# Queries kept once and unscaled, and scaled per head on GpSimd beside the attention

## The chip, the cores and the metric

The kernel runs on one core of a Trainium2 chip. The metric is device time in microseconds (us) of one execution. The core has five engines that run side by side: TensorE (matrix products), VectorE and ScalarE (elementwise work), GpSimd (general), and SyncE, whose queue issues nearly all transfers (DMAs) here.

## The reference

Input x is (8, 1024, 256). The first part is an attention without a softmax: each of 16 heads of 16 dimensions sums five sines of the scaled product of query and key, and a sigmoid makes the weight.

```python
q = (x @ Wq.T + bq).reshape(B, L, H, hd).transpose(0, 2, 1, 3)   # k, v alike
sim = jnp.einsum('bhid,bhjd->bhij', q, k) / jnp.sqrt(hd)
sim = sim / (jnp.abs(temperature)[0] + 0.1)
scores = 0
for fi, freq in enumerate([31.0, 37.0, 41.0, 43.0, 47.0]):
    scores = scores + alpha[:, fi] * jnp.sin(TWO_PI * sim / freq + phi[:, fi])
w = jax.nn.sigmoid(scores)
w = w / (jnp.sum(w, axis=-1, keepdims=True) + 1e-10)
out = layernorm(einsum('bhij,bhjd->bhid', w, v) @ Wo.T + bo) * gamma + beta
x = layernorm(x + out)
```

A second part picks 127 of 1024 rows of each batch entry with a router, runs a transformer block on them, puts them back, and ends with another layer normalization. The change doesn't touch it.

## The kernel before

The program has three blocks, one after the other, which hand data on through HBM: `project_qkv`, `oscillatory_attention`, `routed_block`. Between engines there are semaphores only, each engine's instructions run in the order in which they are written.

**Projections.** A loop over 8 batch entries. TensorE turns x (L200), ScalarE draws it from PSUM (L346), TensorE makes queries and keys (L211) and values (L219). VectorE draws the queries, scaled by temperature (L306), sums x (L310), adds the bias to the values (L318) and splits the keys in a rounded part, the rest and both negated (L326 to L331). The query also has to be divided by each of the five periods and split in a rounded part and a rest, so that products in TensorE's reduced fp32 format (fp32r) stay exact: `split_q` does it on VectorE for five frequencies, with ten operations for each half of the 256 dimensions (L296, L300) and ten writes of 1 MB in all to `q_d`, which has the shape [B, 2, D, NF, L]. SyncE's `keep` issues these writes (L141); each of five buffers is taken again once its write has landed (`q_kept`). A table `tab_d` holds for each head the amplitudes, the reciprocal periods and the phases in two parts.

**Attention.** 128 heads (8 batch entries by 16), one after the other, with two sets of buffers. For a head, `q_r` holds for each frequency and half of the queries 51 rows: 16 dimensions of the rounded part, these again, 16 of the rest, two phase rows and a row of ones. SyncE's `load` brings these rows from `q_d` and from `ph_d`, an array of phase rows made by VectorE at the start, and the keys' rows from `k_d`. `k_r` holds the keys for it, `rounder` the constants by which the sum is brought to a whole number of turns and taken away again. The keys are taken in 8 units of 128. For each unit and frequency TensorE makes one group of eight matmuls into one of three PSUM slots (`fill`, L527; two halves of the array side by side), ScalarE takes the sine (L593), and for each pair of units VectorE sums the five sines, weighted, in four operations (L609). ScalarE turns the sum into a weight with a Tanh (L587), TensorE multiplies by the values (L547), VectorE draws the result (L618). GpSimd only copies a head's five amplitudes (L506).

What orders the work: ScalarE may be at most a pair ahead of VectorE (`summed`: two buffers of sines, and the Tanh of one pair stands before the last sine of the next). TensorE is at most three sines ahead of ScalarE. The loads of a head's keys and queries wait until the fills of the head before last, which used the same buffers, are done (`filled`).

Elsewhere, in the routed block, GpSimd also does a 128x2048 `tensor_tensor` for each batch entry (L800), at times beside VectorE's work (L1087, L1088). These lines serve as a measure below.

Of the kernel before, what the change touches and what calls it, by code (L numbers as in the profile page):

```python
# [15 lines left out]
F32R = mybir.dt.float32r  # L16
# [60 lines left out]
def project_qkv(nc, x, wq, bq, wk, bk, wv, bv, temperature, alpha, phi, q_d, k_d, v_d, vs_d, tab_d):  # L77

    with ExitStack() as ctx:
# [10 lines left out]
        rate = sb("p_rate", [P, KC, NF])  # L90
# [6 lines left out]
        q_hl = sb("p_q_hl", [P, NF, 2, L])  # L97
# [10 lines left out]
        q_kept = [sem(f"q_kept{f}") for f in range(NF)]  # L108
        k_kept, v_kept = sem("k_kept"), sem("v_kept")
        q_step, q_split, k_step, k_split = sem("q_step"), sem("q_split"), sem("k_step"), sem("k_split")  # L110
        tab_in, tab_step, tab_done, tab_kept, rate_in = sem("tab_in"), sem("tab_step"), sem("tab_done"), sem("tab_kept"), sem("rate_in")
        totals, tot_ready, tot_kept = sem("totals"), sem("tot_ready"), sem("tot_kept")

        with nc.Block() as block:

            @block.sync
            def _(sp):
# [9 lines left out]
                for f in range(NF):  # L127
                    sp.sem_inc(q_kept[f], 16)
# [6 lines left out]
                def keep(b):  # L135
                    sp.wait_ge(v_ready, b + 2)
                    sp.dma_start(v_d[b, :, :, :], v_sb[:]).then_inc(v_kept, 16)
                    for m in range(KC):
                        for f in range(NF):
                            sp.wait_ge(q_split, NF * (KC * b + m) + f + 1)  # L140
                            sp.dma_start(q_d[b, :, m * P:(m + 1) * P, f, :].rearrange("i p l -> p i l"),  # L141
                                         q_hl[:, f, :, :]).then_inc(q_kept[f], 16)
# [9 lines left out]
                for m in range(KC):  # L152
                    sp.dma_start(rate[:, m, :], tab_d[8 * m:8 * m + 8, 1, :].unsqueeze(1).broadcast_to([8, HD, NF])).then_inc(rate_in, 16)
# [10 lines left out]
                for f in range(NF):  # L164
                    sp.wait_ge(q_kept[f], 16 * (KC * B + 1))
# [66 lines left out]
            def _(dve):  # L232
# [58 lines left out]
                def split_q(b, m):  # L291

                    whole = qk_sb[:, 0, m, :]
                    for f in range(NF):
# [3 lines left out]
                    for f in range(NF):  # L298
                        dve.wait_ge(q_step, NF * (KC * b + m) + f + 1)
                        nc.vector.scalar_tensor_tensor(q_hl[:, f, 1, :].bitcast(F32R), whole, rate[:, m, f:f + 1],  # L300
                                                       q_hl[:, f, 0, :], ALU.mult, ALU.subtract).then_inc(q_split, 1)

                with dve.Fori(0, B, 1) as b:
                    dve.wait_ge(q_summed, b + 1)
                    for m in range(KC):
# [6 lines left out]
                    dve.wait_ge(q_ready, b + 1)  # L312
                    dve.wait_ge(rate_in, 32)
                    split_q(b, 0)
# [7 lines left out]
                    split_q(b, 1)  # L322
# [35 lines left out]
def oscillatory_attention(nc, tab_d, q_d, k_d, v_d, ph_d, o_d):  # L358
# [3 lines left out]
    HF = H * NF  # L362
    with ExitStack() as ctx:
# [4 lines left out]
        phase = sb("a_phase", [HF, 2])  # L368
        phase_rows = sb("a_phase_rows", [HF, 2, L])
        fixed = sb("a_fixed", [2, 2, L])  # L370
        fixed_m = sb("a_fixed_m", [1, 3, HALF])
# [12 lines left out]
        table_in, phase_step, phase_kept = sem("table_in"), sem("phase_step"), sem("phase_kept")  # L384
        setup, cleared, fixed_in = sem("a_setup"), sem("a_cleared"), sem("a_fixed_in")
        qk_loaded = [sem("qk_loaded0"), sem("qk_loaded1")]
# [27 lines left out]
        LOADS = 16 * 14  # L414
# [11 lines left out]
        with nc.Block() as block:  # L426

            @block.sync
            def _(sp):
                sp.dma_start(table[:],  # L430
                             tab_d[:, 0, :].partition_broadcast(P)).then_inc(table_in, 16)
                for i in range(2):
                    sp.dma_start(phase[:, i:i + 1], tab_d[:, 2 + i, :].rearrange("h (f o) -> h f o", o=1),
                                 allow_slow_non_contiguous=True).then_inc(table_in, 16)
                sp.wait_ge(cleared, 9)
                for j in range(2):
                    at = 64 * j + ONE_ROW
                    for i in range(2):
                        sp.dma_start(rounder[at:at + 1, i, :], fixed_m[:, i, 0:P]).then_inc(fixed_in, 16)
                    for k in range(2):  # L440
                        for i in range(2):
                            sp.dma_start(k_r[64 * j + 48:64 * j + 50, k, i, :], fixed[:, i, :]).then_inc(fixed_in, 16)
                        sp.dma_start(q_r[at:at + 1, k, :, :], fixed_m[:, 2:3, :].broadcast_to([1, NF, HALF])).then_inc(fixed_in, 16)
                sp.wait_ge(phase_step, 2)
                sp.dma_start(ph_d.rearrange("i h f l -> (h f) i l"), phase_rows[:]).then_inc(phase_kept, 16)
                sp.wait_ge(phase_kept, 16)

                def load(g, k):

                    wait_pos(sp, filled, NF * U * (g - 1))  # L450
                    b, h = g // H, g % H
                    to_q = lambda row, count, src: sp.dma_start(q_r[row:row + count, k, :, :], src).then_inc(qk_loaded[k], 16)
# [31 lines left out]
            def _(pool):  # L484
# [7 lines left out]
                for i, value in enumerate((ROUND, -ROUND, 1.0)):  # L492
                    last = nc.gpsimd.memset(fixed_m[:, i, :], value)
# [789 lines left out]
```

## Time and profile before

| | |
|---|---|
| runs shown | 7113.47, 7120.93, 7120.65 us, median 7120.65 |
| profiled execution | 7119.98 us, its span (first to last instruction) 7118.2 us |
| TensorE, matmul | 6113.5 us busy, 86% |
| ScalarE | 5853.0 us, 82% |
| VectorE | 5773.2 us, 81% |
| GpSimd | 205.8 us, 3% |
| moved by DMA | 446.10 MB |

The busy shares are averages over three blocks with different limits; each is to be read by itself. PE is TensorE, DVE VectorE, ACT ScalarE, POOL GpSimd, SP SyncE.

### The profile page before, as it was taken

How to read it: one execution, taken by the hardware profiler on the slowest of the kernel's cores; microseconds unless marked ns; L12 is line 12 of the kernel's file. 1: busy time of each engine (PE TensorE's matmuls, PEld its weight loads, DVE VectorE, ACT ScalarE, POOL GpSimd, SP SyncE). 2: the span in 40 equal slices, each digit the busy share in tenths (PEclk: the TensorE clock that was granted, in tenths of full speed). 3: DMA queues.
4: the chain of work that ended last, by engine and by line, in shares of the span. 5: the costliest groups of instructions: out<-in, count | busy, mean ns of one | idle time of the engine just before them, and what ended most of it. 6: DMA issues, size and time to landing. Idle time of an engine off the chain costs nothing. (4 is left out here: it accounts for less than half of the span.)

```text
span 7118.2 us, 130314 instructions
## 1 busy us (share of the span) xinstructions
PE 6113.5 (86%) x48057; PEld 4363.9 (61%) x48057; DVE 5773.2 (81%) x4353; ACT 5853.0 (82%) x5874; POOL 205.8 (3%) x217
## 2 busy tenths in 40 slices
PE   6539999999999999999999999999999999826555
PEld 3326666666666666666666666666666666625444
DVE  6648888888888888888888888888888888857775
ACT  1139999999999999999999999999999999901111
POOL 0000000000000000000000000000000000010000
PEclk8769999999999999999999999999999999966666
DMA  7931111111111111111111111111111111131220
GB/s 291 358 143 47 47 47 46 46 47 46 45 47 45 45 47 47 47 46 47 46 47 46 47 47 46 47 45 46 47 45 46 47 45 47 30 81 46 50 52 20
DMA packets 322961, 446.10 MB, mean 63 GB/s; under 512 B 158980, under 2 KB 189604, under 8 KB 321384
## 3 DMA queue, kind: packets, MB, share of 16 engines
q1 hardware_dynamic: 317032, 432.81, 19.4%
q8 instruction: 422, 6.91, 0.4%
q0 software_dynamic: 5376, 5.30, 0.3%
q14 instruction: 131, 1.07, 0.0%
HBM read 284.11 MB, written 153.75 MB: 62 GB/s over the span
## 5 line engine op out<-in xcount | busy, mean ns | idle before, releaser
L593 ACT ACTIVATE a_wave<-a_ps_turn 128x1024 f32<-128x1024 f32 x5120 | 4915.0, 1365 | 132.2 <-PE a_ps_turn L527 131.9
L527 PE MATMUL a_ps_turn<-a_q_r,a_k_r 64*128 64x512 f32 x20480 | 3392.0, 399 | 399.8 <-ACT a_wave L593 249.3
L609 DVE SCALAR_TENSOR_TENSOR a_weight<-a_wave,a_head_c,a_weight 128x2048 f32<-128x2048 f32 x1536 | 3612.6, 2352 | 59.5
L527 PE MATMUL a_ps_turn<-a_q_r,a_rounder 64*128 64x512 f32 x20480 | 3241.4, 392 | 4.6 <-issue 4.6
L527 PEld LDWEIGHTS a_ps_turn<-a_q_r,a_k_r 64*128 64x128 f32 x20480 | 1951.8, 185 | 1574.9 <-ACT a_wave L593 804.5
L527 PEld LDWEIGHTS a_ps_turn<-a_q_r,a_rounder 64*128 64x128 f32 x20480 | 1976.6, 186 | 244.6 <-issue 9.4
L609 DVE SCALAR_TENSOR_TENSOR a_weight<-a_wave,a_head_c 128x2048 f32<-128x2048 f32 x512 | 1203.9, 2351 | 844.4 <-ACT a_wave L593 844.4
L587 ACT ACTIVATE a_weight<-a_weight,a_head_c 128x2048 f32<-128x2048 f32 x512 | 1186.0, 2316 | 5.2 <-DVE a_weight L609 5.2
L547 PE MATMUL a_ps_out<-a_weight,a_v_r 128*32 128x512 f32 x4096 | 547.2, 606 | 7.6 <-ACT a_weight L587 5.4
L506 POOL COPY a_head_c<-a_table 128x5 f32 (+1 forms) x128 | 114.3, 893 | 5596.2 <-ACT a_weight L587 5596.1
L547 PEld LDWEIGHTS a_ps_out<-a_weight,a_v_r 128*32 128x32 f32 x4096 | 80.8, 108 | 194.7 <-issue 184.0
L352 ACT ACTIVATE p_qk_sb<-p_lo,p_bias 128x1024 f32<-128x1024 f32 x16 | 16.9, 1110 | 220.1 <-DVE p_k_hl L331 203.8
L219 PE MATMUL p_hi<-p_w_t,p_x_t 128*128 128x256 f32 x256 | 71.0, 446 | 108.0 <-DVE p_qk_sb L306 108.0
L296 DVE TENSOR_SCALAR p_q_hl<-p_qk_sb,p_rate 128x1024 fp32r<-128x1024 f32 x80 | 57.3, 749 | 112.4 <-DMA q_d<-p_q_hl 112.4
L219 PEld LDWEIGHTS p_hi<-p_w_t,p_x_t 128*128 128x128 f32 x256 | 58.0, 230 | 124.2 <-DVE p_qk_sb L306 113.8
L917 PE MATMUL Bk<-ident,logits 128*127 128x128 f32 x128 | 30.3, 431 | 117.9 <-ACT logits L965 117.9
L965 ACT ACTIVATE spread<-spread 128x8 f32<-128x8 f32 x24 | 5.0, 209 | 137.0 <-DVE spread L1052 136.9
L917 PEld LDWEIGHTS Bk<-ident,logits 128*127 128x127 f32 x128 | 27.9, 334 | 120.1 <-ACT logits L965 120.1
L211 PE MATMUL p_hi<-p_x_t,p_w_t 128*128 128x512 f32 x128 | 73.4, 738 | 27.7 <-ACT p_x_t L346 16.9
L300 DVE SCALAR_TENSOR_TENSOR p_q_hl<-p_qk_sb,p_rate,p_q_hl 128x1024 fp32r<-128x1024 f32 x80 | 97.0, 1277 | 0.0
L858 PE MATMUL A<-woa_t,o_t 128*128 128x256 f32 x256 | 69.7, 433 | 27.8 <-DVE o_t L1081 27.8
L618 DVE COPY a_out<-a_ps_out 128x512 f32<-128x512 f32 x128 | 87.4, 683 | 4.1 <-PE a_ps_out L547 4.1
(231 smaller groups left out, 1919.3 us busy)
## 6 DMA issues: line engine op xcount, KB each, us to landing
q_d<-p_q_hl SPq DMA_DIRECT2D x80, 1024.0 KB, 8.3
a_q_r<-q_d SPq DMA_DIRECT2D x256, 320.0 KB
a_k_r<-k_d SPq DMA_DIRECT2D x512, 128.0 KB
a_q_r<-q_d SPq DMA_DIRECT2D x256, 160.0 KB
k_d<-p_k_hl SPq DMA_DIRECT2D x8, 4096.0 KB, 15.2
a_k_r<-k_d SPq DMA_DIRECT2D x512, 64.0 KB
o_d<-a_out SPq DMA_DIRECT2D x512, 34.0 KB
num<-o_d SPq DMA_DIRECT2D x32, 512.0 KB
```

The costliest lines, as they stand in the source:

```text
L211: last = nc.tensor.matmul(out[:, 2 * m + half, :], w_t[:, n, c, m * P:(m + 1) * P], x_t[:, c, half * HALF:(half + 1) * HALF], start=(c == ...
L219: last = nc.tensor.matmul(hi[:, t // 2, (t % 2) * D:(t % 2 + 1) * D], x_t[:, c, t * P:(t + 1) * P], w_t[:, 2, c, :], start=(c == 0), stop= ...
L300: nc.vector.scalar_tensor_tensor(q_hl[:, f, 1, :].bitcast(F32R), whole, rate[:, m, f:f + 1], q_hl[:, f, 0, :], ALU.mult, ALU.subtract).the ...
L506: nc.gpsimd.tensor_copy(head_c[:, k, :], table[:, bass.ds(g % H, 1), :].rearrange("p h f -> p (h f)")).then_inc(const_ready, 1)
L527: last = nc.tensor.matmul(ps_turn[slot_of(r, s, f)][:, half, :], exact(w(rows[half])), exact(q_r[rows[half], k, f, :]), start=(i == 0), st ...
L547: last = nc.tensor.matmul(ps_out[VP * c:VP * (c + 1), :], v_r[:, k, t + c // 2, :], weight[:, t // 2, c // 2, halved(c % 2)], start=(t == ...
L587: nc.scalar.activation(tile, tile, ACT.Tanh, scale=head_c[:, k if s > 1 else 1 - k, 0:1]).then_inc(squashed, 1)
L593: nc.scalar.activation(wave[:, s // 2 % 2, f, s % 2, :], ps_turn[slot_of(r, s, f)][:].rearrange("p a b -> p (a b)"), ACT.Sin, scale=TURN_I ...
L609: return v.scalar_tensor_tensor(both(weight[:, i, :, :]), both(wave[:, i % 2, f, :, :]), head_c[:, k, f:f + 1], to, ALU.mult, ALU.add)
L618: v.tensor_copy(out[:, 1 - k, :], ps_out[:]).then_inc(out_ready, 1)
L858: ins = mm(A[:, 2 + t // 2, (t % 2) * D:(t % 2 + 1) * D], o_t[:, c, half * HALF + t * P:half * HALF + (t + 1) * P], woa_t[:, c, :], start= ...
L917: ins = tr(Bk[0:KSEL, n // 4, (n % 4) * P:(n % 4 + 1) * P], logits[:, n, 0:KSEL], ident[:])
```

## The change

The queries are written once, unscaled: `q_d` becomes [B, D, L], one write of 1 MB for each batch entry, and `split_q` goes from the projections, with its buffers and the `rate` table. In attention a head's 16 rows of queries are loaded three times over into a small tile `q_in`, [P, 2, HALF]; its rows 48 to 50 (and 112 to 114) are ones. A tile `factor` holds for each row and head the five factors by which its row of `q_in` is to be multiplied: the reciprocal periods, the two parts of the phase, and a one. A new `split_q` on GpSimd makes a head's whole `q_r` a head ahead. The phase rows in HBM, VectorE's work for them and their loads go. TensorE waits for `q_ready` beside the keys' loads.

```diff
-                def split_q(b, m):
-
-                    whole = qk_sb[:, 0, m, :]
-                    for f in range(NF):
-                        dve.wait_ge(q_kept[f], 16 * (KC * b + m + 1))
-                        nc.vector.tensor_scalar(q_hl[:, f, 0, :].bitcast(F32R), whole, rate[:, m, f:f + 1], None,
-                                                ALU.mult).then_inc(q_step, 1)
-                    for f in range(NF):
-                        dve.wait_ge(q_step, NF * (KC * b + m) + f + 1)
-                        nc.vector.scalar_tensor_tensor(q_hl[:, f, 1, :].bitcast(F32R), whole, rate[:, m, f:f + 1],
-                                                       q_hl[:, f, 0, :], ALU.mult, ALU.subtract).then_inc(q_split, 1)
...
+                    for k in range(2):
...
+                        sp.dma_start(q_in[64 * j + 48:64 * j + ONE_ROW + 1, k, :], fixed[0:1, 0:1, 0:HALF].broadcast_to([1, 3, HALF])).then_inc(fixed_in, 16)
+                    sp.dma_start(factor[64 * j:64 * j + 48, :, :], tab_d[:, 1, :].partition_broadcast(48)).then_inc(table_in, 16)
+                    for i in range(2):
+                        sp.dma_start(factor[64 * j + 48 + i:64 * j + 49 + i, :, :], tab_d[:, 2 + i, :].partition_broadcast(1)).then_inc(table_in, 16)
+                    sp.dma_start(factor[at:at + 1, :, :].rearrange("p h f -> p (h f)"), fixed[0:1, 0, 0:H * NF]).then_inc(table_in, 16)
...
                 def load(g, k):
+                    wait_pos(sp, q_taken, g - 1)
+                    for j in range(2):
+                        sp.dma_start(q_in[64 * j:64 * j + 48, k, :],
+                                     q_d[b, dims, halved(j)].unsqueeze(0).broadcast_to([3, HD, HALF])).then_inc(q_loaded[k], 16)
                     wait_pos(sp, filled, NF * U * (g - 1))
...
-                        to_q(64 * j, 2 * HD, q_d[b, 0:1, dims, :, halved(j)].broadcast_to([2, HD, NF, HALF]))
-                        to_q(64 * j + 2 * HD, HD, q_d[b, 1, dims, :, halved(j)])
-                        to_q(64 * j + 3 * HD, 2, ph_d[:, head, :, halved(j)].rearrange("i o f l -> i (o f) l"))
...
+                def split_q(g, k):
+
+                    nc.gpsimd.tensor_copy(rate[:, k, :], factor[:, bass.ds(g % H, 1), :].rearrange("p h f -> p (h f)")).then_inc(rate_ready, 1)
+                    pool.wait_ge(rate_ready, g + 1)
+                    pool.wait_ge(q_loaded[k], q_loads(g, k))
+                    whole = q_in[:, k, :].unsqueeze(1).broadcast_to([P, NF, HALF])
+                    scale = rate[:, k, :].unsqueeze(2).broadcast_to([P, NF, HALF])
+                    nc.gpsimd.tensor_tensor(q_all[:], whole, scale, ALU.mult).then_inc(q_step, 1)
+                    wait_pos(pool, filled, NF * U * (g - 1))
+                    nc.gpsimd.tensor_tensor(q_r[:, k, :, :].bitcast(F32R), whole, scale, ALU.mult).then_inc(q_taken, 1)
+                    pool.wait_ge(q_step, g + 1)
+                    pool.wait_ge(q_taken, g + 1)
+                    for j in range(2):
+                        low = slice(64 * j + 32, 64 * j + 48)
+                        last = nc.gpsimd.tensor_tensor(q_r[low, k, :, :].bitcast(F32R), q_all[low, :, :], q_r[low, k, :, :], ALU.subtract)
+                    last.then_inc(q_ready, 1)
+                    pool.wait_ge(q_ready, g + 1)
...
                 def body(g, k):
                     if not isinstance(g, int) or g + 1 < HEADS:
+                        split_q(g + 1, 1 - k)
                         constants(g + 1, 1 - k)
...
-                dve.wait_ge(table_in, 48)
-                for i in range(2):
-                    v.tensor_copy(phase_rows[:, i, :].bitcast(F32R), phase[:, i:i + 1].broadcast_to([HF, L])).then_inc(phase_step, 1)
```

## Rows read from the trace of the kernel before

**Rows 1.** The page: busy tenths of each engine in 40 equal slices.

```profile
PE   6539999999999999999999999999999999826555
DVE  6648888888888888888888888888888888857775
ACT  1139999999999999999999999999999999901111
```

**Rows 2.** Windows: one head, attention, its cold start, projections (batch 0, later), attention's preparation.

```profile
core 0: us, PE busy (x) PEld busy (x) DVE busy (x) ACT busy (x) POOL busy (x), PEclk, DMA share, GB/s
1015.77:1059.95 44.18, 42.22 (x356) 29.73 (x352) 38.24 (x18) 44.18 (x45) 0.91 (x2) 1.00 0.16 47
...
473.20:479.00 5.80, 5.80 (x28) 4.94 (x30) 0.00 (x0) 2.32 (x3) 0.00 (x0) 0.50 0.24 71
20.52:48.78 28.26, 24.88 (x81) 14.73 (x81) 16.47 (x17) 5.28 (x4) 0.00 (x0) 1.00 0.11 41
240.00:285.00 45.00, 26.59 (x80) 15.90 (x79) 31.74 (x30) 5.28 (x4) 0.00 (x0) 0.77 0.94 364
412.40:473.20 60.80, 0.00 (x0) 0.03 (x1) 2.45 (x2) 1.49 (x2) 13.35 (x14) 0.50 0.18 46
473.20:6220.60 5747.40, 5438.35 (x45052) 3836.26 (x45056) 4892.58 (x2175) 5660.49 (x5632) 113.95 (x126) 0.99 0.16 46
```

**Rows 3.** Timeline of one pair: start us, us, engine, line, operation [idle before].

```profile
1011.90 2.35 DVE L609 SCALAR_TENSOR_TENSOR a_weight<-a_wave,a_head_c 128x2048 f32<-128x2048 f32 x1 [1.52 <-ACT a_wave L593]
...
1014.29 7.12 DVE L609 SCALAR_TENSOR_TENSOR a_weight<-a_wave,a_head_c,a_weight 128x2048 f32<-128x2048 f32 x3
...
1015.77 0.91 POOL L506 COPY a_head_c<-a_table 128x5 f32 x1 [43.25 <-ACT a_weight L587]
```

**Rows 4.** The page, projections: groups (busy us, mean ns | idle), and DMA issues.

```profile
L296 DVE TENSOR_SCALAR p_q_hl<-p_qk_sb,p_rate 128x1024 fp32r<-128x1024 f32 x80 | 57.3, 749 | 112.4 <-DMA q_d<-p_q_hl 112.4
...
L300 DVE SCALAR_TENSOR_TENSOR p_q_hl<-p_qk_sb,p_rate,p_q_hl 128x1024 fp32r<-128x1024 f32 x80 | 97.0, 1277 | 0.0
...
q_d<-p_q_hl SPq DMA_DIRECT2D x80, 1024.0 KB, 8.3
...
k_d<-p_k_hl SPq DMA_DIRECT2D x8, 4096.0 KB, 15.2
```

**Rows 5.** Timeline of the first batch's projections, TensorE.

```profile
20.52 9.36 PE L211 MATMUL p_hi<-p_x_t,p_w_t 128*128 128x512 f32 x16 [3.39 <-ACT p_x_t L346]
...
43.49 1.91 PE L200 MATMUL p_lo<-p_ident,p_x_in 128*128 128x128 f32 x16
48.78 8.83 PE L211 MATMUL p_hi<-p_x_t,p_w_t 128*128 128x512 f32 x16 [3.38 <-ACT p_x_t L346]
```

**Rows 6.** Timeline, one small issue on SyncE's queue before attention.

```profile
430.52 0.73 SPq L443 DMA_DIRECT2D a_q_r<-a_fixed_m  x1
```

**Rows 7.** Timeline in the routed block, GpSimd beside VectorE.

```profile
6349.89 1.37 POOL L819 DMA_INDIRECT m_row<-in_L_ffn_attention_mask,mask_row  x1 [0.17 <-issue]
...
6350.51 5.45 DVE L1087 TENSOR_TENSOR den<-den 128x128 f32<-128x128 f32 x1
6351.30 4.51 POOL L800 TENSOR_TENSOR x_in<-x_in,rows 128x2048 f32<-128x2048 f32 x1
```

**Rows 8.** Groups of GpSimd's instructions: busy us, mean ns | idle before.

```profile
L783 POOL TENSOR_SCALAR_AFFINE_SELECT spot<-spot 128x1024 f32<-128x1024 f32 x2 | 3.0, 1518 | 0.0
```

**Rows 9.** Tile a_head_c: duration ns min/median/max, first and last start.

```profile
L609 DVE SCALAR_TENSOR_TENSOR a_weight<-a_wave,a_head_c,a_weight x1536: 2350/2352/2355, 486.2 to 6216.0; 128x2048 f32<-128x2048 f32 x192
...
L506 POOL COPY a_head_c<-a_table x128: 178/903/1222, 425.9 to 6135.1; 128x5 f32 x122, 128x5 f32<-128x5 f32 x6
```

**Rows 10.** Lines L1087 and L1088: duration ns min/median/max.

```profile
L1087 DVE TENSOR_TENSOR den<-den x8: 291/292/5449, 6272.1 to 6946.4; 128x128 f32<-128x128 f32 x8
...
L1088 DVE TENSOR_SCALAR den<-den x8: 226/226/4401, 6272.4 to 6946.7; 128x128 f32<-128x128 f32 x8
```

**Rows 11.** Timeline of attention's first sines on ScalarE.

```profile
477.02 1.02 ACT L593 ACTIVATE a_wave<-a_ps_turn 128x1024 f32<-128x1024 f32 x1 [0.68 <-PE a_ps_turn L527]
```

More of the change, by code:

```diff
@@ L107, in project_qkv @@
         q_ready, k_ready, v_ready = sem("q_ready"), sem("k_ready"), sem("v_ready")
[L108 to L111, printed above, removed]
+        q_kept, k_kept, v_kept = sem("q_kept"), sem("k_kept"), sem("v_kept")
+        k_step, k_split = sem("k_step"), sem("k_split")
+        tab_in, tab_step, tab_done, tab_kept = sem("tab_in"), sem("tab_step"), sem("tab_done"), sem("tab_kept")
         totals, tot_ready, tot_kept = sem("totals"), sem("tot_ready"), sem("tot_kept")
@@ L135, in keep @@
                 def keep(b):
+                    sp.wait_ge(q_ready, b + 1)
+                    sp.dma_start(q_d[b, :, :].rearrange("(m p) l -> p m l", p=P), qk_sb[:, 0, :, :]).then_inc(q_kept, 16)
                     sp.wait_ge(v_ready, b + 2)
                     sp.dma_start(v_d[b, :, :, :], v_sb[:]).then_inc(v_kept, 16)
-                    for m in range(KC):
-                        for f in range(NF):
-                            sp.wait_ge(q_split, NF * (KC * b + m) + f + 1)
-                            sp.dma_start(q_d[b, :, m * P:(m + 1) * P, f, :].rearrange("i p l -> p i l"),
-                                         q_hl[:, f, :, :]).then_inc(q_kept[f], 16)
                     sp.wait_ge(k_split, b + 2)
@@ L163, in _ @@
                 sp.dma_start(vs_d[:, :, :], v_tot[:]).then_inc(tot_kept, 16)
-                for f in range(NF):
-                    sp.wait_ge(q_kept[f], 16 * (KC * B + 1))
+                sp.wait_ge(q_kept, 16 * (B + 1))
                 sp.wait_ge(k_kept, 16 * (B + 1))
@@ L289, in _ @@
                 flat = lambda ap: ap.rearrange("p m l -> p (m l)")
[L291 to L301 removed]
                 with dve.Fori(0, B, 1) as b:
                     dve.wait_ge(q_summed, b + 1)
+                    dve.wait_ge(q_kept, 16 * (b + 1))
                     for m in range(KC):
@@ L367, in oscillatory_attention @@
         table = sb("a_table", [P, H, NF])
-        phase = sb("a_phase", [HF, 2])
-        phase_rows = sb("a_phase_rows", [HF, 2, L])
+        factor = sb("a_factor", [P, H, NF])
+        rate = sb("a_rate", [P, 2, NF])
+        q_in = sb("a_q_in", [P, 2, HALF])
+        q_all = sb("a_q_all", [P, NF, HALF])
         fixed = sb("a_fixed", [2, 2, L])
-        fixed_m = sb("a_fixed_m", [1, 3, HALF])
+        fixed_m = sb("a_fixed_m", [1, 2, P])
         rounder = sb("a_rounder", [P, 2, P])
@@ L491, in _ @@
                 pool.wait_ge(setup, 1)
-                for i, value in enumerate((ROUND, -ROUND, 1.0)):
+                for i, value in enumerate((ROUND, -ROUND)):
                     last = nc.gpsimd.memset(fixed_m[:, i, :], value)
```

55 lines of the change are left out of this document (23 added, 32 removed).

## The prediction

> **What bounds the kernel now.** I read the page by slices first [rows 1]. Three stages show: slices 1 to 3 (projections), slices 4 to 35 (attention) and the last five (routed block). In the middle stage ScalarE and TensorE are at 9 tenths and VectorE at 8, so three engines lie close together. The windows [rows 2] put numbers on it: in one head of 44.18 us ScalarE is busy for all of it, TensorE for 42.2 and VectorE for 38.2; the whole attention stage takes 5747.4 us, 44.9 us for each of 128 heads. ScalarE sets the pace and VectorE has 6 us of slack. The reader should see how thin that is: anything that takes more than some 6 us from VectorE in a head makes VectorE the bound.
>
> The timeline of one pair of key blocks [rows 3] shows how. VectorE does four scalar_tensor_tensor of 128x2048 (one of 2.35 us, then three in 7.12), then waits 1.5 us for a sine. With the hand-overs a pair is 9.55 us of VectorE against 11.04 of ScalarE (a quarter of a head). A head is 38.2 us busy [rows 2] plus 16 gaps of 0.035, so 38.8 us of VectorE.
>
> In the projections the windows show 45 us for a batch, DMA at 0.94 and 364 GB/s, TensorE at 27 us and VectorE at 32 [rows 2]. VectorE's scaled queries wait 112 us for the writes of the scaled queries, 80 of 1 MB each [rows 4]. DMA bounds this stage.
>
> **What is removed.** In a batch, ten scalings and ten subtractions, (57.3 + 97.0) / 8 = 19.3 us of VectorE [rows 4], and nine of ten MB written, 9.4 MB. Of 364 GB/s x 45 us = 16.4 MB that leaves 7.0 MB, 19 us. VectorE keeps 31.7 - 19.3 = 12.4 us. What is late next is TensorE's chain with ScalarE's draw of the turned input: batch 0, where no write had yet filled the queue, ran from 20.52 to the next batch's first matmul at 48.78, 28.26 us, TensorE 24.9 busy at full clock [rows 2, 5]. Eight such batches from 20.5, less the last batch's turning and draw (1.9 + 3.4 [rows 5]), end at 241.3. Some two thirds of VectorE's 12.4 us (adding to values, splitting keys) follow, 8.3, and the last keys' write, 15.2 to landing [rows 4]: 264.8. The stage ended at 412.4 before, so **-147.6 us**. Bounds: at DMA's 19 us for a batch it would be another -74; if TensorE stays at the later window's clock of 0.77 [rows 2], its 24.9 us become 32.3 and the gain falls to -88.
>
> The 256 loads of scaled queries of 320 and 256 of 160 KB and the phase loads go too, three SyncE issues of each half for one small one. DMA in a head is at 0.16 [rows 2] and no head waits for it: 0 us, hidden behind 44 us of ScalarE.
>
> **The start of attention** took 60.8 us before the first matmul [rows 2]. Clearing falls from 13.4 to about 8.8 us on GpSimd (5120 columns become 1104). SyncE then issues 24 small DMAs for 16, at about 0.68 (one shown is 0.73 [rows 6]): 16.3. The phase rows' way through HBM is gone. New on the path are the first query load (1.4 to issue, about 4 to land) and GpSimd's split of head 0, 16.8 as below. Sum 47.3, so **-13.5 us** (-8 with the long subtraction).
>
> **What is added.** For each head GpSimd does one 5-column copy, two products 128x2560 and two subtractions of 16 partitions by 2560. A two-input tensor_tensor on GpSimd took 4.51 us at 2048 columns [rows 7]: 2.2 ns a column, 5.6 us at 2560. GpSimd's own time, 17 to 22 us in a head of 44, has room, and the queries are ready a head ahead of TensorE. If that were all, it would cost 0.
>
> It is not all. The trace of before shows the two engines stopping each other. GpSimd's 5-column copy is 178 ns at the least and 903 in the median [rows 9]: the one at 1015.77 started within a VectorE operation begun at 1014.29, and ended at 1016.68, within 0.04 us of that operation's end at 1016.64 [rows 3]. In the other direction, VectorE's 128x128 tensor_tensor, 292 ns in the median, took 5449 ns once [rows 10]: begun at 6350.51, it ended at 6355.96, just behind GpSimd's two-input product (6351.30 + 4.51 = 6355.81) [rows 7]. A one-input operation beside another such product was stretched from 226 to 4401 ns [rows 10]. So a GpSimd product holds VectorE for its whole length, and attention's 16 operations have the same form, two inputs in SBUF.
>
> The page "SBUF — State Buffer" of the Trainium skill, section Who interferes with whom, says the same against this change: a VectorE instruction with two SBUF inputs and a GpSimd instruction that reads SBUF exclude each other for their full length. By that rule, the trace agrees, with 5449 ns for 292.
>
> The holds per head are two products, 11.2 us, and the subtractions. These touch partitions 32 to 47 and 96 to 111, with no wait between them. No row shows two such operations. Bounds: 5.6 (side by side) and 11.2 (in turn). The nearest is the same stretch [rows 7]: VectorE's short operation was held from 6350.51, though the product is shown only from 6351.30, behind an indirect DMA; something of the product may already have run. That speaks weakly for GpSimd work overlapping, and I take 5.6: holds of 16.8 us.
>
> The page "GPSIMD Engine Reference" of the skill, section Instruction dispatch, says that each of eight cores serves 16 partitions and starts the next instruction when its own share is done; by it the holds would be 16.8 too. No row here can show it.
>
> Now VectorE is the bound: 38.8 + 16.8 = 55.6 us. On top comes what it still waits for ScalarE: in the pairs without a hold it works at 11.04 instead of 9.55, 1.5 us each. Two such pairs would give 3.0, against 0 if the holds leave ScalarE far enough ahead. I take 2.4: **58.0 us per head**. 128 x 58.0, less the 16.8 the last head has no use for, is 7407 us, against 5747: **+1660 us**. The odd 0.7 us between 44.18 and 44.9 lies within ScalarE's new idle time.
>
> Sum: 7118.2 - 147.6 - 13.5 + 1660 = 8617.1, and with the 1.8 us that lie around the span 8619. The profiled execution, 7119.98, is 0.7 below the median of the runs, 7120.65. So +21%. About 0.2% is what a measurement of this kernel can tell from no change.
>
> **Rivals.**
> (a) The subtractions run in turn: 5.6 us more in each of 128 splits, +717: 9336 us. For it: all other GpSimd operations in the trace follow one another. Against: the held operation above.
> (b) The products are cheaper, because an operand that repeats isn't fetched for each column. A one-input selection of 1024 columns took 1.5 us [rows 8], 3.75 at 2560. Holds 7.5 + 5.6 = 13.1, head 54.3: 8149 us.
> (c) The other side: VectorE isn't held. GpSimd takes the port only in VectorE's gaps, or attention's operation goes through while a product waits. Then both savings stand alone: 7118.2 - 161.1 + 1.8 = 6959 us. It decides as soon as holds are under 6.1 us of slack plus 161 / 128 = 1.3, so 7.4 us in a head. For it: in 126 heads GpSimd's copy waited and VectorE's 2352 ns never moved (2350 to 2355) [rows 9]; but that copy is too short to hold anything. Against: the held operations [rows 7, 10].
> (d) TensorE's clock. It was granted 0.50 of full speed, 1.2 GHz, when it began after 61 us of idleness [rows 2], and a group of eight matmuls then took 1.70 us [rows 11] where ScalarE asks for one each 0.96. A head at this level would be 40 x 1.70 + 4 x 2.1 = 76 us, above 58: about 10,900 us. It decides if the mean granted clock falls under 42.2 / 58 = 0.73. Against: TensorE stays busy over 70% and ScalarE stops only for some 8 us at a time. A short dip at half clock, for which ScalarE has spare time, costs nothing in my sum.
> (e) No difference. The change does what it says, but gain and loss cancel: that takes the 7.4 us of holds named in (c), which no row gives.
>
> **How the numbers follow.** Forecast 0.50, (a) 0.23, (b) 0.13, (c) 0.08, (d) 0.04, (e) within 0.2% 0.02. The forecast's own range is 8310 (no wait for ScalarE) to 8750. The range reaches to (b) at 8140 and to (a) with 0.8 us more of waits, 9440; it leaves out (c), (d), (e) and some. Faster 0.08, same 0.02, slower 0.90.
>
> **What would show it.** In the profile after: VectorE's scalar_tensor_tensor with a median near 2352 but a mean well above (16.8 us over 16: about 3.4 us), maxima near 8; GpSimd's products near 5.6 plus up to 2.35 of waiting; ScalarE's busy share in attention down to 0.76, VectorE's nearly 1; period of a head 58. The two subtractions starting within 0.2 us of each other speak for 16.8, one 5.6 behind the other for (a). Attention's first matmul near 312, not 473. TensorE's clock in the windows of attention near 0.9 or above; below 0.73 it is (d). The prediction is wrong if VectorE's operations keep 2352 as their mean.

## The result, and the profile of the changed kernel

The changed kernel takes 9022.88 us (median of four runs, 9016.48 to 9023.65) against 7117.99 in runs beside them: a ratio of 1.2675, interval [1.2653, 1.2697]. The forecast was 8619 us, 8140 to 9440. Direction and range hold, and the point is 4.5% low. The range holds only because it reaches to rival (a): the forecast's own part of it, 8310 to 8750, doesn't contain the result. The profiled execution (9016.48, span 9014.7) is used below.

From the page, busy time of each engine, then tenths of it in 40 slices, as in [rows 1]:

```profile
PE 6392.0 (71%) x48057; PEld 4661.3 (52%) x48057; DVE 7894.1 (88%) x4191; ACT 5916.5 (66%) x5874; POOL 3696.2 (41%) x857
...
PE   8577777777777777777777777777777777764555
...
DVE  4599999999999999999999999999999999976776
ACT  1477777777777777777777777777777777771111
POOL 0444544444444454444445445444444544520000
```

ScalarE and TensorE fall from 9 tenths to 7 and VectorE rises to 9: in attention VectorE is now the bound. The windows (columns as in [rows 2]) of projections, the start of attention, attention, one head, and three stretches of that head:

```profile
20.00:256.00 236.00, 194.51 (x632) 115.55 (x632) 104.20 (x82) 39.31 (x31) 0.00 (x0) 0.90 0.62 237
256.70:308.00 51.30, 0.00 (x0) 0.02 (x1) 0.00 (x0) 1.49 (x2) 27.80 (x18) 0.50 0.19 42
308.00:8086.00 7778.00, 5736.27 (x45056) 4146.21 (x45056) 7149.61 (x2175) 5723.95 (x5632) 3589.75 (x763) 0.87 0.07 20
3038.00:3099.30 61.30, 45.00 (x354) 32.00 (x353) 56.06 (x17) 44.68 (x45) 28.17 (x7) 0.86 0.07 20
3048.00:3064.00 16.00, 5.47 (x48) 3.47 (x44) 15.93 (x3) 3.13 (x4) 15.38 (x3) 0.81 0.05 18
3064.00:3076.00 12.00, 7.28 (x38) 5.74 (x40) 11.04 (x5) 8.25 (x8) 2.24 (x2) 0.55 0.00 0
3076.00:3087.00 11.00, 10.85 (x94) 7.77 (x93) 9.35 (x5) 11.00 (x12) 0.00 (x0) 1.00 0.07 7
```

Attention takes 7778 us, 60.8 a head (this head 61.3), where it was 5747 [rows 2]. The first matmul comes at 308.0 instead of 473.2. VectorE does the same 2175 operations as before and is busy for 7149.6 us instead of 4892.6. The page's groups show on which, with what GpSimd now does:

```profile
L608 DVE SCALAR_TENSOR_TENSOR a_weight<-a_wave,a_head_c,a_weight 128x2048 f32<-128x2048 f32 x1536 | 5453.0, 3550 | 59.9 <-DVE a_weight L608 0.5
...
L608 DVE SCALAR_TENSOR_TENSOR a_weight<-a_wave,a_head_c 128x2048 f32<-128x2048 f32 x512 | 1630.1, 3184 | 627.4 <-ACT a_wave L596 627.4
L491 POOL TENSOR_TENSOR a_q_all<-a_q_in,a_rate 128x2560 f32<-128x2560 f32 x128 | 572.9, 4476 | 3489.2 <-DMA a_q_in<-q_d 3489.1
L498 POOL TENSOR_TENSOR a_q_r<-a_q_all,a_q_r 16x2560 fp32r<-16x2560 f32 x256 | 1919.0, 7496 | 25.8
L493 POOL TENSOR_TENSOR a_q_r<-a_q_in,a_rate 128x2560 fp32r<-128x2560 f32 x128 | 827.6, 6466 | 26.4 <-PE a_ps_turn L528 26.4
```

VectorE's sums (L608) take (5453.0 + 1630.1) / 128 = 55.3 us a head instead of 16 x 2.35 = 37.6. That is 17.7 us of holds. GpSimd's means hold its own waiting too. The timeline just before the first matmul, with VectorE idle, shows its operations alone (start, length):

```profile
287.67 4.46 POOL L491 TENSOR_TENSOR a_q_all<-a_q_in,a_rate 128x2560 f32<-128x2560 f32 x1 [4.02 <-DMA a_q_in<-q_d]
292.08 4.45 POOL L493 TENSOR_TENSOR a_q_r<-a_q_in,a_rate 128x2560 fp32r<-128x2560 f32 x1
296.68 11.19 POOL L498 TENSOR_TENSOR a_q_r<-a_q_all,a_q_r 16x2560 fp32r<-16x2560 f32 x2
```

A product takes 4.45 us, not 5.6. The two subtractions take 11.19 us together: in turn, 5.6 each. The same in the head of the window, GpSimd and VectorE:

```profile
3037.43 4.46 POOL L491 TENSOR_TENSOR a_q_all<-a_q_in,a_rate 128x2560 f32<-128x2560 f32 x1 [28.30 <-DMA a_q_in<-q_d]
3041.84 6.51 POOL L493 TENSOR_TENSOR a_q_r<-a_q_in,a_rate 128x2560 fp32r<-128x2560 f32 x1
3048.50 15.08 POOL L498 TENSOR_TENSOR a_q_r<-a_q_all,a_q_r 16x2560 fp32r<-16x2560 f32 x2
```

```profile
3038.29 5.75 DVE L608 SCALAR_TENSOR_TENSOR a_weight<-a_wave,a_head_c 128x2048 f32<-128x2048 f32 x1 [1.53 <-ACT a_wave L596]
3044.07 21.65 DVE L608 SCALAR_TENSOR_TENSOR a_weight<-a_wave,a_head_c,a_weight 128x2048 f32<-128x2048 f32 x3
3065.65 2.34 DVE L608 SCALAR_TENSOR_TENSOR a_weight<-a_wave,a_head_c 128x2048 f32<-128x2048 f32 x1
...
3077.55 2.35 DVE L608 SCALAR_TENSOR_TENSOR a_weight<-a_wave,a_head_c 128x2048 f32<-128x2048 f32 x1 [2.40 <-ACT a_wave L596]
```

The engines alternate. VectorE's first operation waits for L491's end (2.35 becomes 5.75), the next three take 21.65 us instead of 7.13, and each of GpSimd's later operations waits up to 2.1 us for the VectorE operation in progress (6.51 - 4.45; 15.08 - 11.19 for two). ScalarE's timeline shows what that does further on:

```profile
3041.66 9.47 ACT L596 ACTIVATE a_wave<-a_ps_turn 128x1024 f32<-128x1024 f32 x10
3065.76 2.00 ACT L590 ACTIVATE a_weight<-a_weight,a_head_c 128x2048 f32<-128x2048 f32 x1 [14.63 <-DVE a_weight L608]
3067.67 2.83 ACT L596 ACTIVATE a_wave<-a_ps_turn 128x1024 f32<-128x1024 f32 x3
3070.84 1.02 ACT L596 ACTIVATE a_wave<-a_ps_turn 128x1024 f32<-128x1024 f32 x1 [0.34 <-PE a_ps_turn L528]
3072.55 1.02 ACT L596 ACTIVATE a_wave<-a_ps_turn 128x1024 f32<-128x1024 f32 x1 [0.68 <-PE a_ps_turn L528]
3074.26 1.02 ACT L596 ACTIVATE a_wave<-a_ps_turn 128x1024 f32<-128x1024 f32 x1 [0.68 <-PE a_ps_turn L528]
3075.56 3.79 ACT L596 ACTIVATE a_wave<-a_ps_turn 128x1024 f32<-128x1024 f32 x4 [0.28 <-PE a_ps_turn L528]
```

ScalarE fills its buffers and stands for 14.6 us, TensorE with it (5.5 us busy in 16). For the 12 us behind it TensorE's granted clock is 0.55, close to the lower level of 1.2 GHz, and for a while sines come 1.71 us apart. The ten sines from 3067.67 on take 11.7 us; the ten of the next pair, at full clock, take 9.25. VectorE, just released, then waits for a sine, 2.40 us here. So a head is 38.8 us of VectorE's own + 17.7 of holds + 4.4 of waiting ((627.4 less one wait of 72.4 before the first head) / 127) = 60.9.

### The profile page after: what moved, and what is told of

It reads as the page before. It is cut to its first block and busy times, and to the rows that moved or that the text cites. A ratio compares the mean times of both kernels' runs of the same rounds, so it can differ in the third digit from the quotient of the medians.

```text
span 9014.7 us, 129841 instructions
## 1 busy us (share of the span) xinstructions
PE 6392.0 (71%) x48057; PEld 4661.3 (52%) x48057; DVE 7894.1 (88%) x4191; ACT 5916.5 (66%) x5874; POOL 3696.2 (41%) x857
## 5 line engine op out<-in xcount | busy, mean ns | idle before, releaser
L608 DVE SCALAR_TENSOR_TENSOR a_weight<-a_wave,a_head_c,a_weight 128x2048 f32<-128x2048 f32 x1536 | 5453.0, 3550 | 59.9 <-DVE a_weight L608 0.5
L528 PE MATMUL a_ps_turn<-a_q_r,a_k_r 64*128 64x512 f32 x20480 | 3577.6, 417 | 2100.1 <-ACT a_wave L596 1972.7
L528 PEld LDWEIGHTS a_ps_turn<-a_q_r,a_k_r 64*128 64x128 f32 x20480 | 2079.8, 195 | 3193.0 <-ACT a_wave L596 2486.8
L528 PE MATMUL a_ps_turn<-a_q_r,a_rounder 64*128 64x512 f32 x20480 | 3405.9, 409 | 0.0
L528 PEld LDWEIGHTS a_ps_turn<-a_q_r,a_rounder 64*128 64x128 f32 x20480 | 2116.3, 197 | 310.5 <-issue 0.9
L608 DVE SCALAR_TENSOR_TENSOR a_weight<-a_wave,a_head_c 128x2048 f32<-128x2048 f32 x512 | 1630.1, 3184 | 627.4 <-ACT a_wave L596 627.4
L491 POOL TENSOR_TENSOR a_q_all<-a_q_in,a_rate 128x2560 f32<-128x2560 f32 x128 | 572.9, 4476 | 3489.2 <-DMA a_q_in<-q_d 3489.1
L498 POOL TENSOR_TENSOR a_q_r<-a_q_all,a_q_r 16x2560 fp32r<-16x2560 f32 x256 | 1919.0, 7496 | 25.8
L493 POOL TENSOR_TENSOR a_q_r<-a_q_in,a_rate 128x2560 fp32r<-128x2560 f32 x128 | 827.6, 6466 | 26.4 <-PE a_ps_turn L528 26.4
L486 POOL COPY a_rate<-a_factor 128x5 f32 (+1 forms) x128 | 271.4, 2120 | 34.0 <-DMA a_factor<-a_fixed 17.5
```

The costliest lines, as they stand in the source:

```text
L486: nc.gpsimd.tensor_copy(rate[:, k, :], factor[:, bass.ds(g % H, 1), :].rearrange("p h f -> p (h f)")).then_inc(rate_ready, 1)
L491: nc.gpsimd.tensor_tensor(q_all[:], whole, scale, ALU.mult).then_inc(q_step, 1)
L493: nc.gpsimd.tensor_tensor(q_r[:, k, :, :].bitcast(F32R), whole, scale, ALU.mult).then_inc(q_taken, 1)
L498: last = nc.gpsimd.tensor_tensor(q_r[low, k, :, :].bitcast(F32R), q_all[low, :, :], q_r[low, k, :, :], ALU.subtract)
L528: last = nc.tensor.matmul(ps_turn[slot_of(r, s, f)][:, half, :], exact(w(rows[half])), exact(q_r[rows[half], k, f, :]), start=(i == 0), st ...
L608: return v.scalar_tensor_tensor(both(weight[:, i, :, :]), both(wave[:, i % 2, f, :, :]), head_c[:, k, f:f + 1], to, ALU.mult, ALU.add)
```

## The experiments

The theory: GpSimd's reads of SBUF hold VectorE for their whole length, all four operations of a head in turn. The rivals: the cost lies in something else of the change (the loads in front of a head, TensorE's wait for `q_ready`, the clock by itself), or in GpSimd's being busy, whatever it does. Except for the two versions at the end, each experiment is a single run; the runs of the kernel before beside them took 7110 to 7127 us.

**The split left out** (the loads, the waits and the start stay):

```diff
-                    nc.gpsimd.tensor_tensor(q_all[:], whole, scale, ALU.mult).then_inc(q_step, 1)
...
+                    if isinstance(g, int) and g < 2:
...
+                    else:
+                        nc.gpsimd.tensor_tensor(tiny[:, 1:2], tiny[:, 0:1], tiny[:, 0:1], ALU.mult).then_inc(q_step, 1)
```

> The changed kernel with GpSimd's two products and two subtractions left out for heads 2 to 127 (three 1-column operations pass the semaphores on; these heads are computed from the first two heads' queries). All loads, waits and the new projections stay. Theory (GpSimd's reads hold VectorE): attention returns to 44.9 us a head, and only the savings in front stand: 154 us in the projections and 11 at the start of attention, so 7118 - 165 = 6955 us, within 30. Rival 1 (the new loads, waits or their order cost the time): it stays near 9020. Rival 2 (TensorE's lower clock is a cause and not a result): the clock stays at 0.84 and the time well above 7000; the theory wants 0.93 or more.

Measured 6999.65 us (before: 7124.27). Its windows for attention, and VectorE's operations (ns, min/median/max, the maximum from the first two heads, which are still split):

```profile
308.00:6064.00 5756.00, 5448.58 (x45056) 3870.52 (x45056) 4903.05 (x2175) 5660.62 (x5632) 601.84 (x637) 0.99 0.10 27
```

```profile
L619 DVE SCALAR_TENSOR_TENSOR a_weight<-a_wave,a_head_c,a_weight x1536: 2350/2352/7631, 319.7 to 6058.6; 128x2048 f32<-128x2048 f32 x192
```

Attention is back at 5756 us, before 5747, at a clock of 0.99. The whole loss lies in the four operations: the loads, the waits and the clock cost nothing without them. Savings ahead of attention are real, 165 us to the first matmul, but the total is only 125 below, 45 us above what was expected. Some 8 us of that are in attention and 37 in the routed block, which the edit doesn't touch: from attention's last draw (L628) it takes 933 us, before 896.

**What kind of work holds VectorE.** In place of the split, four memsets of 128x5120, which write but read nothing, or eight one-input copies of 128x2560:

```diff
+                        nc.gpsimd.memset(idle[:].rearrange("p i l -> p (i l)"), 0.0).then_inc(idled, 1)
```

```diff
+                        nc.gpsimd.tensor_copy(idle[:, 1, :], idle[:, 0, :]).then_inc(idled, 1)
```

> As the run without the split, but GpSimd clears a 128x5120 tile four times in each head, 4.4 us each, 17.5 us of work which reads nothing from SBUF; 1-column operations stand between them. Theory (what holds VectorE is the read side that the two share): 6955 us, within 50, and VectorE's operations stay near 2352 ns. Rival (any GpSimd work holds VectorE, or its writes do): some 44.9 - 6.1 + 17.5 = 56 us a head, 8400 us or more.

> As the run without the split, but GpSimd copies a 128x2560 tile eight times in each head: operations with one input read from SBUF. What one takes is not known from the traces, between 2.2 us (the rate of clearing) and 3.8 (the rate of a selection), 17.6 to 30 us in a head. Theory (any read of SBUF by GpSimd holds VectorE): a head takes 38.8 + 17.6 to 30 us, so 8400 to 9900 us. Rival (only operations with two inputs hold it): 6955 us.

Measured 7004.63 and 8254.18 us. Groups of the first, then of the second:

```profile
L633 DVE SCALAR_TENSOR_TENSOR a_weight<-a_wave,a_head_c,a_weight 128x2048 f32<-128x2048 f32 x1536 | 3617.9, 2355 | 59.9 <-DVE a_weight L633 0.5
...
L519 POOL MEMSET a_idle<- 128x5120 f32 x126 | 553.1, 4389 | 0.0
```

```profile
L646 DVE SCALAR_TENSOR_TENSOR a_weight<-a_wave,a_head_c,a_weight 128x2048 f32<-128x2048 f32 x1536 | 5425.7, 3532 | 59.6 <-DVE a_weight L646 0.5
L646 DVE SCALAR_TENSOR_TENSOR a_weight<-a_wave,a_head_c 128x2048 f32<-128x2048 f32 x512 | 1436.5, 2806 | 107.3 <-ACT a_wave L634 107.3
...
L523 POOL COPY a_idle<-a_idle 128x2560 f32<-128x2560 f32 x126 | 293.2, 2327 | 0.0
```

Writing for 4 x 4.39 = 17.6 us a head leaves VectorE's mean at 2355 ns: being busy isn't it. Eight copies of 2.33 us, 18.6 in all, add (5425.7 + 1436.5) / 128 - 37.6 = 16.0 us. The total is 146 us under the least that was expected, 8400, which had counted a hold of 17.6. Reading is what counts, and one input is enough. The page "SBUF — State Buffer" of the Trainium skill, section Who interferes with whom, draws the same line for a VectorE instruction with two SBUF inputs: it contends with a GpSimd instruction that reads SBUF and not with one that only writes it. These two runs agree.

**One subtraction instead of two** (the rows of one half's low part keep the second product):

```diff
-                    for j in range(2):
+                    for j in range(2 if isinstance(g, int) and g < 2 else 1):
```

> The changed kernel without the second of the two subtractions (partitions 96 to 111; the low part of the second half of the queries isn't formed). Theory (holds add one to one): 5.6 us less in each head, 9020 - 126 x 5.6 = 8315 us, within 80. Rival (the two were held up together by a cause outside them, the clock or a late load): under 300 us less.

Measured 8287.87 us. Attention took 7041 us instead of 7778: 737 / 126 = 5.85 us for each head. A subtraction on 16 partitions costs its full 5.6 us and a little waiting: rival (a) of the prediction is shown, and nothing of it is side by side.

**Why a product is cheaper than a subtraction.** The subtraction was first made a multiplication, everything else kept:

```diff
-                        last = nc.gpsimd.tensor_tensor(q_r[low, k, :, :].bitcast(F32R), q_all[low, :, :], q_r[low, k, :, :], ALU.subtract)
+                        last = nc.gpsimd.tensor_tensor(q_r[low, k, :, :].bitcast(F32R), q_all[low, :, :], q_r[low, k, :, :], ALU.mult if g_late(g) else ALU.subtract)
```

> The changed kernel with the two subtractions replaced by multiplications of the same operands from head 2 on (so that the low part of the queries is a product there). In the changed kernel's trace the products take 4.46 us at 2560 columns and the subtractions 5.56. Theory 1 (the operation makes the difference): 4.46 each, 2.2 us less in a head, 9020 - 126 x 2.2 = 8743 us. Theory 2 (the products are cheaper because their operands repeat, and a subtraction reads two full ones): 5.56 each and no change, 9020 within 30.

Measured 9023.89 us, with the tile's row almost that of the change:

```profile
L500 POOL TENSOR_TENSOR a_q_r<-a_q_all,a_q_r x256: 5562/7525/7693, 297.4 to 7986.4; 16x2560 fp32r<-16x2560 f32 x128
```

The arithmetic isn't it. Three causes were left, so ten forms were run by themselves in the kernel before, ahead of VectorE's first sum, with VectorE idle (the cut shows the second form):

```diff
+                for i in range(3):
+                    nc.gpsimd.tensor_tensor(spare[:, 2, :], spare[:, 0, :], spare[:, 1, :], ALU.mult).then_inc(extra_done, 1)
+                    pool.wait_ge(extra_done, 3 + i + 1)
```

> The kernel before, with thirty extra two-input operations of 2560 columns on GpSimd at the start of attention, three of each of ten forms, on a spare tile of ones (nothing of the computation is left out; it starts some 150 us later, so the total says nothing). In order: one tensor with itself; two different ones; the same subtracted; two different ones with the result written over the second; a full one with five repeated factors; both repeated (the form of the change's products); one repeated with a full one; then on 16 partitions: two different ones; one with itself; two different ones with the result written over the second (the form of the change's subtractions). Theory 1 (the two columns' values have to be fetched separately, a repeated or common operand is cheaper): 4.45 us for the first, fifth, sixth, seventh and ninth, 5.56 for the second, third, fourth, eighth and tenth. Theory 2 (the result over an input makes it dear): 5.56 for the fourth and tenth alone, 4.45 for all others. Theory 3 (16 partitions make it dear): 5.56 for the last three alone. The product of the routed block, 4.51 us at 2048 columns, has two different inputs and its result over one of them, so it speaks against theory 3 and not between 1 and 2.

The tile's rows (ns, min/median/max), in the order of the text above:

```profile
L509 POOL TENSOR_TENSOR a_spare<-a_spare x3: 4452/4452/4452, 431.8 to 440.8; 128x2560 f32<-128x2560 f32 x3
L512 POOL TENSOR_TENSOR a_spare<-a_spare x3: 5569/5571/5572, 445.4 to 456.7; 128x2560 f32<-128x2560 f32 x3
...
L518 POOL TENSOR_TENSOR a_spare<-a_spare x3: 5709/5750/5753, 479.3 to 490.9; 128x2560 f32<-128x2560 f32 x3
L521 POOL TENSOR_TENSOR a_spare<-a_spare x3: 4455/4455/4458, 496.7 to 505.8; 128x2560 f32<-128x2560 f32 x3
L524 POOL TENSOR_TENSOR a_spare<-a_spare x3: 4455/4455/4455, 510.3 to 519.4; 128x2560 f32<-128x2560 f32 x3
L527 POOL TENSOR_TENSOR a_spare<-a_spare x3: 5346/5346/5347, 523.9 to 534.8; 128x2560 f32<-128x2560 f32 x3
L530 POOL TENSOR_TENSOR a_spare<-a_spare x3: 5562/5562/5562, 540.2 to 551.5; 16x2560 f32<-16x2560 f32 x3
L533 POOL TENSOR_TENSOR a_spare<-a_spare x3: 4443/4444/4444, 557.1 to 566.1; 16x2560 f32<-16x2560 f32 x3
L536 POOL TENSOR_TENSOR a_spare<-a_spare x3: 5562/5562/5562, 570.7 to 581.9; 16x2560 f32<-16x2560 f32 x3
```

Nine of ten came as theory 1 said, the fourth 0.18 us dearer. The price goes by the operands: 1.74 ns a column when both are the same data or one is a factor that stays for 512 columns, 2.17 with two different ones, and the number of partitions changes neither (4452 and 4444, 5571 and 5562). Writing over an input adds 0.18 us on 128 partitions and nothing on 16. The miss is the seventh form: a short row that comes again and again beside a full one is at 5.35 us nearly as dear as two full ones. The runs show how the price goes with the form, not why. The product of the routed block [rows 7], from which the prediction took its rate, is of the dear kind: a row of 256 columns repeated beside a full operand, written over the full one.

**One extra product in the kernel before.** A 128x2560 product of a spare tile with itself for each head, all else as it was:

```diff
+                    for i in range(1):
+                        nc.gpsimd.tensor_tensor(spare[:, 1, 0:2560], spare[:, 0, 0:2560], spare[:, 0, 0:2560], ALU.mult).then_inc(extra_done, 1)
```

> The kernel before, with one GpSimd product of two full inputs, 128x2560, added in each head, on data that nobody reads: a hold of 5.6 us at one place. Theory A, as the prediction had it (what counts is VectorE's slack over a head, 6.1 us): no change, within 30 us of 7118. Theory B (what counts is how long VectorE may be late at one place: in the trace of before the sum of a pair is ready 2.85 us before ScalarE's Tanh asks for it, and VectorE waits up to 1.5 us before a pair): 5.6 - 1.5 to 2.85 us is passed on to ScalarE in each head, 2.8 to 4.1 us, so +350 to +520 us.

Measured 7261.23 us, +142: neither expectation. The expectation spoke of two full inputs and 5.6 us, but the edit has one tensor twice, which takes 4.45 (the first form above); with it theory B gives +200 to +375, still too much. The timeline of a head, and the group of each pair's first operation:

```profile
1033.22 11.35 DVE L618 SCALAR_TENSOR_TENSOR a_weight<-a_wave,a_head_c,a_weight 128x2048 f32<-128x2048 f32 x3
```

```profile
L618 DVE SCALAR_TENSOR_TENSOR a_weight<-a_wave,a_head_c 128x2048 f32<-128x2048 f32 x512 | 1202.3, 2348 | 486.4 <-ACT a_wave L602 486.4
```

Three operations take 11.35 us where 7.13 is usual: a hold of 4.2 us. So hold and price of the product agree (4.2 and 4.45), and what was wrong is what a hold leaves for the time: 142 / 127 = 1.1 us a head. VectorE's slack of some 6 us is not there for one hold. It lies in four waits of 1.5 us, and a hold in one place can be made up only from the waits near it, as far as ScalarE's two buffers reach. VectorE's waits for sines are 486.4 us in all, where the same group of the kernel before has 844.4: 2.8 us less a head. 4.2 less 2.8 is 1.4, near the 1.1. That sum was made after the run.

**The same work in short pieces.** The 2560 columns as four operations of 640, one in each pair of key blocks:

```diff
+                    for i in range(4):
+                        wait_pos(pool, summed, 4 * g + i)
+                        nc.gpsimd.tensor_tensor(spare[:, 1, 640 * i:640 * (i + 1)], spare[:, 0, 640 * i:640 * (i + 1)], spare[:, 0, 640 * i:640 * (i + 1)], ALU.mult).then_inc(extra_done, 1)
```

> The kernel before, with the same 2560 columns of products a head as four of 128x640, 1.4 us each, each released by the sum of another pair. Theory A and B both: no change, within 30 us of 7118 (1.4 us at a place is under 1.5 + 2.85). Rival (each hold costs its length, wherever it stands): 127 x 5.6 = +710 us.

Measured 7125.27 us (before: median 7119.36 of 7 runs, up to 7127.23): no change. The group's row:

```profile
L619 DVE SCALAR_TENSOR_TENSOR a_weight<-a_wave,a_head_c 128x2048 f32<-128x2048 f32 x512 | 1312.6, 2564 | 617.4 <-ACT a_wave L603 617.4
```

VectorE is still held, (3741.8 + 1312.6) / 128 - 37.6 = 1.9 us a head (3741.8 is the other group's), and it costs nothing: the waits for sines shrink by as much, from 844.4 us to 617.4, 1.8 a head. The amount of reading is that of the run above. It is cut in four and spread at once, and the two together make the difference of 136 us; no run separates them.

**The change's own operations on VectorE** instead of GpSimd, ahead of the second pair of a head:

```diff
-                    nc.gpsimd.tensor_tensor(q_all[:], whole, scale, ALU.mult).then_inc(q_step, 1)
+                    v.tensor_tensor(q_all[:], whole, scale, ALU.mult).then_inc(q_step, 1)
```

> The changed kernel with the same two products and two subtractions of 2560 columns a head on VectorE instead of GpSimd, after the first pair of a head. VectorE took 0.82 us for 640 columns, so 2.75 us each, 11.0 us a head, in a row. Theory (GpSimd's holds cost VectorE their whole length, and VectorE needs half of it for the same work): a head takes 38.8 + 11.0 = 49.8 us and up to 1.8 more, as 11 us in a row are more than one place bears: 7118 - 165 + 31 + 127 x (4.9 to 6.7) = 7610 to 7840 us, faster than the change by over 1100. Rival (GpSimd relieves VectorE of at least a part): 9000 or more.

Measured 7849.64 us, 10 above the top of what was expected. The timeline of a head:

```profile
3015.48 2.82 DVE L603 TENSOR_TENSOR a_q_all<-a_q_in,a_rate 128x2560 f32<-128x2560 f32 x1
3018.21 2.82 DVE L605 TENSOR_TENSOR a_q_r<-a_q_in,a_rate 128x2560 fp32r<-128x2560 f32 x1
3021.14 5.65 DVE L610 TENSOR_TENSOR a_q_r<-a_q_all,a_q_r 16x2560 fp32r<-16x2560 f32 x2
```

Four times 2.82 is 11.3 us of VectorE, less than the 17.7 that it loses while GpSimd does them. A head takes 6651.4 / 128 = 52.0 us. The work moved off VectorE costs VectorE 6.4 us more a head than it would by doing it, and with the waits behind it some 1120 us of attention; the other 50 of the 1173 between the two kernels lie before and behind it. It is still 10% slower than before: for one head, with its 16 dimensions on few partitions or several times over, the split takes 11.3 us, in the projections it was 19.3 for a batch of 16 heads.

**Two versions that keep the saving.** Queries stored once and unscaled, as in the change. Batch entry 0 is split in the projections as before; the other seven are split during attention, 128 rows by 128 columns of one batch ahead for each head, on 128 partitions, in three operations of 640 columns, and written to `q_d` as before. In the first VectorE does them, the two products ahead of the second pair of a head and the subtraction ahead of the fourth, where it would wait; in the second GpSimd does all three in a row. The cut shows the second.

```diff
+                def high_part(g, k):
+                    each = piece[:, k, :].unsqueeze(1).broadcast_to([P, NF, P])
+                    by = rate[:, k, :].unsqueeze(2).broadcast_to([P, NF, P])
+                    nc.gpsimd.tensor_tensor(whole[:], each, by, ALU.mult).then_inc(piece_prod, 1)
...
+                    nc.gpsimd.tensor_tensor(parts[:, k, 0, :, :].bitcast(F32R), each, by, ALU.mult).then_inc(piece_high, 1)
...
+                    nc.gpsimd.tensor_tensor(parts[:, k, 1, :, :].bitcast(F32R), whole[:], parts[:, k, 0, :, :], ALU.subtract).then_inc(piece_low, 1)
```

> The kernel before with the queries stored once and unscaled, but split by VectorE during attention, 16 heads ahead, in pieces which fill all 128 partitions with different dimensions: for each head two products and a subtraction of 128x640, 0.7 us each, and a write of 0.66 MB back to the array of split queries. Only the first batch entry is split in the projections. Its loads and phase rows are those of before. 2.2 us a head, in two places, is under VectorE's slack; the projections end near 272 us instead of 412, so 7118 - 140 = 6978 us, faster by 2%. If the routed block takes the 31 us more that it takes in the changed kernel: 7009. Rival (VectorE has no room between its waits, or the added DMAs delay the loads): above 7100.

> The same with the three operations of a piece on GpSimd, in a row: holds of 1.1, 1.1 and 1.4 us a head instead of 20. By theory B this is about what a place can bear (1.5 + 2.85 us): 6978 us, up to 100 more. Rival (GpSimd beside VectorE costs whatever its length): 127 x 3.6 = 460 us more than with VectorE's own operations less their 2.2: about 7150.

Measured 7017.42 us, ratio 0.9856 [0.9839, 0.9872], and 6991.06 us, ratio 0.9823 [0.9807, 0.984]. They take 1.4% and 1.8% less than the kernel before, a small gain but outside the noise, and beat the changed kernel by far. The groups of the pieces, on VectorE and on GpSimd:

```profile
L674 DVE TENSOR_TENSOR a_whole<-a_piece,a_rate 128x640 f32<-128x640 f32 x112 | 91.7, 819 | 0.0
```

```profile
L563 POOL TENSOR_TENSOR a_whole<-a_piece,a_rate 128x640 f32<-128x640 f32 x112 | 365.0, 3259 | 48.0 <-DMA a_piece<-qw_d 48.0
```

GpSimd's stand 3.3 us, where the shortest takes 1.25; the rest is waiting for VectorE. From the first matmul (at 337.5 and 336.2) to the last draw attention takes 5747 us in both, as before (5749), so the short pieces cost it nothing on either engine. GpSimd's hold VectorE for 2.3 us a head, and VectorE's own three operations take 2.5: GpSimd relieves it of next to nothing. The difference between the two versions lies in the routed block (932 and 896 us in the profiled executions), so it says nothing for GpSimd.

## Why the prediction was right in direction and 4.5% low

Each item names a term as it was forecast, then what was measured.

- **Projections, -147.6 us.** Attention's block began at 258.3 instead of 412.6: -154. A batch takes 27.7 us; the step (TensorE's chain becomes the pace, not DMA's 19 us) was right.
- **Start of attention, -13.5.** -11 (49.7 against 60.6). The first matmul came at 308.0, forecast near 312.
- **The hold itself.** Right: GpSimd's reads stop attention's operations for their length. Rival (c) falls.
- **The step that failed: the subtractions side by side, 5.6 us.** They run in turn, 11.2, as rival (a) has it. The only row for an overlap was a short stretch behind an indirect DMA [rows 7], while every other row showed GpSimd's operations one after another. The page "GPSIMD Engine Reference" of the Trainium skill, section Instruction dispatch, has each core start the next instruction when its own share is done, by which the two would overlap; the 11.19 us here disagree, and the measurement decides.
- **The products, 5.6 each.** 4.45: part of rival (b) holds too, though not its 3.75. The rate came from an operation of another operand form.
- **Holds, 16.8.** By durations 2 x 4.45 + 11.2 = 20.1, of which 17.7 fell on VectorE's work; the rest fell in its waits. The errors, +5.6, -2.3 and -2.4, nearly cancel: that 16.8 came so close to 17.7 is luck.
- **The wait for ScalarE, 2.4.** 4.4. The step saw only the pace of ScalarE. It had ScalarE stop "only for some 8 us at a time"; it stops for 14.6, TensorE with it, and TensorE comes back at half clock (0.55 granted over 12 us, 7.3 of them busy). The prediction had the dip as one "for which ScalarE has spare time"; in the head shown ten sines take 2.4 us longer, and VectorE waits for them. That is about the 2.0 us between 4.4 and 2.4; no run isolates the clock. Rival (d) as a whole falls: the mean is 0.87, above 0.73.
- **The routed block, no change.** +31 us (8086 to 9014.7 is 929, before 897.6). VectorE's waits show a candidate, one at the head of each turn of the loop (total us, times, longest):

```profile
DVE den L1086 <- issue: 21.0, 6, 4.5
```

In the kernel before this wait is 2.2 us in all. It is 21 to 22 in the first five experiments, 21.6 and 18.4 in the last two versions, and 2.2 in the kernel before with extra products. It doesn't follow the unscaled queries: the run with the split on VectorE stores them too, and has 2.2 again. Nor does it settle the block's length. Counted from attention's last draw, that is 896 us before, 928 after, 893 with the split on VectorE, 932 and 896 in the last two versions, so the last one has the wait and not the length. None of these kernels edits the block, and what lengthens it stays open. In one turn GpSimd's product also held an operation of 8 columns for 4.53 us.

Added to the forecast: 8619 + 371 (attention 7778 for 7407) + 31 - 4 (first matmul) = 9017, against 9016.5 profiled. Of attention's 371, (17.7 - 16.8) + (4.4 - 2.4) = 2.9 us a head is all but 3.

## What to carry to other kernels

Before work that reads SBUF goes to GpSimd beside a VectorE that reads two SBUF inputs, count it as VectorE's time at GpSimd's duration: it pays only if it is short enough to fall into VectorE's waits, piece by piece, and if VectorE would need about as long itself, VectorE should do it. Slack that a profile shows as a sum per head is not slack for one long hold; look at how it is spread and how deep the buffers are. And do elementwise work where it fills all partitions: the same split cost 11.3 us of VectorE for one head laid out by its 16 dimensions, 19.3 for sixteen heads on 128 different rows, and 2.5 a head in pieces of 128 rows during attention.

## What the runs showed of the hardware that was not expected

- GpSimd's two-input operation has prices that go by the operands' form: 4.45 us at 2560 columns with the same data twice or with a factor held for 512 columns, 5.57 with two different operands, 5.35 with a repeated row of 512 beside a full one; writing over an input adds 0.18 on 128 partitions. Partitions (16 or 128) and operation (multiply, subtract) change nothing beyond 0.02 us.
- Two operations on disjoint groups of 16 partitions, with no wait between them, take 11.19 us, each 5.6.
- GpSimd's short reading operations beside VectorE cost attention nothing where long ones do: one of 4.45 us a head cost 142 us over 127 heads, four of 1.25 nothing.
- A one-input copy of 2560 columns takes GpSimd 2.33 us and holds VectorE too: (5425.7 + 1436.5) / 128 - 37.6 = 16.0 us of 18.6.
- TensorE, at 0.81 in a stretch of 16 us in which it was busy for 5.5, was granted 0.55 in the next 12 and 1.00 in the 11 after these.
